# Cross attention in a decoder layer: transposing each head's probabilities as two row tiles, and a new order inside a slot

## What is computed

```python
q = _split_heads(query @ Wq.T + bq)          # 8 x 16 heads x 112 x 16
k = _split_heads(key @ Wk.T + bk)            # 8 x 16 heads x 375 x 16
v = _split_heads(value @ Wv.T + bv)
scores = jnp.einsum('bhqd,bhkd->bhqk', q, k) * scale
scores = jnp.where(mask == 0, NEG_INF, scores)
probs = jax.nn.softmax(scores, axis=-1)
out = jnp.einsum('bhqk,bhkd->bhqd', probs, v)
return out.transpose(0, 2, 1, 3).reshape(query.shape[0], -1, D_MODEL) @ Wo.T + bo
x = _layernorm(x + that)
```

## Time and profile before

| | |
|---|---|
| median of three runs | 433.10 us |
| profiled execution | 433.16 us |
| its span from first to last instruction | 431.4 us |
| TensorE busy with matmuls | 410.7 us, 95% |
| VectorE busy | 243.3 us, 56% |
| ScalarE busy | 193.9 us, 45% |
| cross attention, from 161.7 us on, to the last values at 328.4 us | about 167 us |

### The profile page before, as it was taken

How to read it: one execution, slowest core, us unless ns; L and a number is a source line. 1 busy time by engine, 2 the same in 40 slices (tenths; PEclk the granted TensorE clock), 3 DMA queues, 4 the chain that set the end, 5 groups by cost and what they waited for, 6 DMA issues and landing times.

```text
span 431.4 us, 8964 instructions
## 1 busy us (share of the span) xinstructions
PE 410.7 (95%) x3128; PEld 296.3 (69%) x3129; DVE 243.3 (56%) x724; ACT 193.9 (45%) x580; POOL 51.0 (12%) x77
## 2 busy tenths in 40 slices
PE   8999999999999979999999999999989999999992
PEld 7767879778796856776776676676665475666661
DVE  1275765747466566666675667666764642244443
ACT  1164362443526446677566666666683101111220
POOL 4010010100101001000010101010100054212222
PEclk9999999999999999999999999999999999999998
DMA  8999000000000013040404040920000013112210
GB/s 246 374 388 260 6 2 2 0 2 2 1 2 0 2 37 147 2 183 2 184 2 183 11 175 7 364 107 2 2 2 2 1 62 98 57 59 65 70 41 27
DMA packets 15242, 34.25 MB, mean 79 GB/s; under 512 B 2382, under 2 KB 9151, under 8 KB 13921
## 3 DMA queue, kind: packets, MB, share of 16 engines
q1 hardware_dynamic: 13952, 30.72, 20.4%
q0 software_dynamic: 1104, 2.76, 1.8%
q10 hardware_dynamic: 144, 0.23, 0.2%
HBM read 27.27 MB, written 6.70 MB: 79 GB/s over the span
## 4 chain that ended last, share of the span: by engine, by line
PE 88%; DVE 5%; ACT 4%; issue 2%; POOL 0%; POOLq 0%; DVEq 0%; ACTq 0%
PE bank L434 11%; PE bank L633 11%; PE bank L448 7%; PE bank L615 6%; PE bank L504 6%; PE bank L809 6%; PE bank L532 5%; PE bank L649 4%; PE bank L899 4%; PE bank L875 4%; PE bank L881 4%; PE bank L526 4%; PE bank L465 3%; PE bank L491 3%; PE bank L821 3%; PE bank L477 3%
## 5 line engine op out<-in xcount | busy, mean ns | idle before, releaser
L1255 DVE CUSTOM_DVE_ANT_0 p<-bank,mask 112x375 f32<-112x375 f32 x128 | 62.6, 544 | 36.5 <-PE bank L615 36.5
L1015 ACT ACTIVATE p<-p,nm 112x375 f32<-112x375 f32 x128 | 74.8, 609 | 2.0 <-DVE nm L1255 2.0
L633 PEld LDWEIGHTS bank<-ident,p 112*125 112x125 f32 x384 | 48.9, 187 | 22.9 <-issue 14.5
L1022 ACT ACTIVATE pT<-bank 125x336 f32<-125x336 f32 x96 | 42.9, 448 | 46.0 <-PE bank L633 46.0
L633 PE MATMUL bank<-ident,p 112*125 112x112 f32 x384 | 58.8, 286 | 1.0
L434 PE MATMUL bank<-x2T,arena 128*128 128x224 f32 x256 | 53.6, 357 | 0.0
L958 ACT ACTIVATE p<-bank,nm 112x112 f32<-112x112 f32 x128 | 43.7, 366 | 18.3 <-DVE nm L1126 18.2
L434 PEld LDWEIGHTS bank<-x2T,arena 128*128 128x128 f32 x256 | 47.0, 192 | 0.6 <-DMA x2T<-in_xT 0.5
L349 POOL TENSOR_TENSOR rstd<-veps,minus_half 128x1 f32<-128x1 f32 x14 | 7.7, 551 | 290.4 <-DVE veps L1152 290.4
L1126 DVE TENSOR_REDUCE nm<-bank 112x4 f32<-112x448 f32 x32 | 19.1, 619 | 24.1 <-PE bank L465 24.1
L615 PE MATMUL bank<-kT,qz 32*112 32x375 f32 x256 | 28.8, 517 | 3.6 <-ACT x2T L984 2.1
(11 more groups left out here) (143 smaller groups left out, 593.0 us busy)
## 6 DMA issues: line engine op xcount, KB each, us to landing
arena<-in_ug SPq DMA_DIRECT2D x8, 1024.0 KB, 5.6
arena<-in_dn SPq DMA_DIRECT2D x8, 512.0 KB, 6.8
mid<-in_ctxT SPq DMA_DIRECT2D x8, 375.0 KB, 3.1
slots_s<-blank SPq DMA_DIRECT2D x14, 128.5 KB, 3.9
arena<-in_wqk SPq DMA_DIRECT2D x7, 256.0 KB, 6.1
slots_x<-blank SPq DMA_DIRECT2D x14, 128.0 KB, 7.2
p<-slots_s SPq DMA_DIRECT2D x9, 128.5 KB, 2.0
kT<-slots_x SPq DMA_DIRECT2D x9, 128.0 KB, 2.1
```

Of the source, the lines that this page charges most:

```text
L633: mm = pe.transpose(PE_T2[r][0:SK, t * S:(t + 1) * S], p2[i % RING][:, t * SK:(t + 1) * SK], ident[0:S, 0:S])
L1015: act.activation(p2[i % RING], p2[i % RING], ACT.Exp, bias=nm2[:, i % H:i % H + 1], scale=-1.0).then_inc(exp2, 1)
L1022: act.activation(pT2[0:SK, i % RING], PE_T2[r][0:SK, 0:KT * S].rearrange("p (k n) -> p k n", k=KT), ACT.Copy).then_inc(pt2_act, 1)
L1255: v.tensor_tensor_reduce(p2[i % RING], PE_S2[r][0:S, 0:S2], bias[:], 1.0, 3e38, ALU.add, ALU.min, accum_out=nm2[:, i % H:i % H + 1]).then_ ...
```

## The change

Four things are changed, all in the cross attention and the few microseconds behind it.

1. Each transpose becomes two: queries 0 to 63 in the upper half of the array's rows (row tile at 0), queries 64 to 111 in the lower half (row tile at 64). The two write to different banks. A slot has 24 transposes in place of 12. Heads are taken in pairs `p`: pair 0 uses banks 4 and 7, pair 1 banks 0 and 1, and a bank holds one half of two heads: 2 x 3 x 64 = 384 columns or 2 x 3 x 48 = 288.
2. ScalarE evacuates both 64-query halves and one 48-query half, VectorE the other 48-query half.
3. The order in a slot is now scores, values, all transposes, all fills. ScalarE's order is: exponentials 0 and 1, two evacuations, exponential 2, an evacuation, exponential 3, and then evacuations of fills.
4. Two fills of the first sequence and the query projections use a second lent score bank, bank 3 (`PE_R2`), and the scores wait for these too. The first part of the second layer norm on VectorE is split: the addition stays at the start of a sequence's first slot, the moments go to the end of that slot. Behind the last slot, parts of the shared expert's first matmuls stand between the remaining steps, and the router's first logits come later.

```diff
-        PE_T2 = (bank[4], bank[7], PE_S2[0], PE_S2[1])
-        PE_L2 = PE_S2[2]
+        PE_T2 = ((bank[4], bank[7]), (PE_S2[0], PE_S2[1]))
+        PE_L2, PE_R2 = PE_S2[2], PE_S2[3]
+        HALVES = ((0, 64), (64, S))
...
-            def turn2_(n, r):
-                pe.wait_ge(exp2, n * STRIPS + r + 1)
+            def turn2_(n, p):
+                pe.wait_ge(exp2, n * STRIPS + 2 * p + 2)
...
+                elif p == 0:
+                    pe.wait_ge(pt2_act, 3 * n)
                 elif n + 1 < SLOTS:
-                    pe.wait_ge(max2, (n + 1) * STRIPS + r - 1)
-                i = n * STRIPS + r
-                for t in range(KT):
-                    mm = pe.transpose(PE_T2[r][0:SK, t * S:(t + 1) * S], p2[i % RING][:, t * SK:(t + 1) * SK], ident[0:S, 0:S])
+                    pe.wait_ge(max2, (n + 1) * STRIPS + 2)
+                for j in range(2):
+                    i = n * STRIPS + 2 * p + j
+                    for t in range(KT):
+                        for half, (q0, q1) in enumerate(HALVES):
+                            at = (j * KT + t) * (q1 - q0)
+                            mm = pe.transpose(PE_T2[p][half][0:SK, at:at + q1 - q0],
+                                              p2_all[q0:q1, (i % RING) * S2 + t * SK:(i % RING) * S2 + (t + 1) * SK],
+                                              ident[q0:q1, q0:q1])
                 mm.then_inc(turn2, 1)
...
+                if g == 1:
+                    pe.wait_ge(x1t_sb, 3)
+                    turn_x1(3)
+                    pe.wait_ge(max2, 4 * STRIPS // 2)
+                    turn_x1(4, PE_R2)
...
                 if n >= 2:
-                    pe.wait_ge(pt2_act, (n - 1) * 3)
+                    pe.wait_ge(pt2_act, 3 * (n - 2) + 2)
                     pe.wait_ge(pt2_dve, n - 1)
...
+                if g == 2 and b in (2, 4):
+                    pe.wait_ge(q_sb, b // 2 + 2)
+                if g in (2, 3) and b == 0:
+                    pe.wait_ge(x1t_sb, g + 3)
...
             for n in range(SLOTS):
                 score2(n)
+                if n >= 2:
+                    value2(n - 2)
                 if n >= 1:
                     turn2_(n - 1, 0)
                     turn2_(n - 1, 1)
-                between(n, 0)
-                if n >= 1:
-                    turn2_(n - 1, 2)
-                    turn2_(n - 1, 3)
-                between(n, 1)
-                between(n, 2)
-                if n >= 2:
-                    value2(n - 2)
+                fills(n)
...
+            shared(0, 0, range(0, 1))
             value2(SLOTS - 1)
-            logits_first()
+            shared(0, 0, range(1, 2))
+            turn_x2(NT - 2, bank[1])
             pe.wait_ge(y2, NT - 1)
             turn_o(B - 1)
-            shared(0, 0, range(0, 1))
+            shared(0, 1, range(0, 1))
             turn_on(B - 1)
-            shared(0, 0, range(1, 2))
+            shared(0, 1, range(1, 2))
+            logits_first()
             out2(NT - 1)
-            shared(0, 1)
             shared(1, 0)
...
             for n in range(SLOTS):
-                before_exps(n)
+                exps2(n, 0)
+                exps2(n, 1)
                 if n >= 1:
                     evac_pt(n - 1, 0)
-                exps2(n, 0)
+                    evac_pt(n - 1, 1)
+                amid(n)
+                exps2(n, 2)
                 if n >= 1:
-                    evac_pt(n - 1, 1)
-                exps2(n, 1)
-                between(n, 0)
-                if n >= 1:
-                    evac_pt(n - 1, 2)
-                exps2(n, 2)
-                between(n, 1)
+                    evac_pt(n - 1, 0, 1)
                 exps2(n, 3)
+                after(n)
...
                 if (g, place) == (0, 0) and b >= 3:
-                    ln2_a(b - 3)
+                    ln2_add(b - 3)
                 if (g, place) == (0, 3) and b >= 1:
                     evac_v(2, b, PE_L2)
+                if (g, place) == (0, 4) and b >= 3:
+                    ln2_a(b - 3)
```

More of the change, by code:

```diff
@@ L690, in between_first, with fills @@
                     project_q(1)
-                if (g, place) == (2, 2):
+                    pe.wait_ge(max2, 3 * STRIPS)
+                    turn_x1(5, PE_R2)
+                if g == 3:
                     pe.wait_ge(q_sb, 2)
-                    turn_x1(5)
-                if (g, place) == (3, 0):
-                    pe.wait_ge(x1t_sb, 6)
                     turn_x1(6)
-            def between(n, place):
+            def fills(n):
                 b, g = n // GROUPS, n % GROUPS
-                if place == 1:
+                if (g == 0 and b >= 1) or (g >= 2 and b + 1 < B) or (g == 1 and b >= 3):
@@ L731, in between @@
-                if (g, place) == (2, 1) and b + 1 < B:
-                    project_v(0, b + 1, PE_L2)
-                if (g, place) == (3, 0) and b >= 1:
-                    turn_on(b - 1)
-                if (g, place) == (3, 1) and b + 1 < B:
-                    project_v(1, b + 1, PE_L2)
-                if (g, place) == (3, 2) and b >= 2:
-                    out2(b - 2)
+                if g == 0 and b >= 1:
+                    project_v(2, b, PE_L2)
+                    if b + 1 < B:
+                        if b == 1:
+                            pe.wait_ge(x1t_sb, NT)
+                        elif b == 2:
+                            pe.wait_ge(ont_sb, 1)
+                        else:
+                            pe.wait_ge(y2, b - 2)
+                        project_k(0, b + 1)
@@ new lines, in fills @@
+                if g == 1 and b >= 1:
+                    if b >= 3:
+                        turn_x2(b - 3)
+                    if b in (2, 4):
+                        pe.wait_ge(max2, n * STRIPS + 4)
+                        project_q(b // 2 + 1, PE_R2)
+                    if b + 1 < B:
+                        pe.wait_ge(k_sb, (b + 1) * KC + 1)
+                        project_k(1, b + 1)
+                if g == 2:
+                    if b + 1 < B:
+                        project_v(0, b + 1, PE_L2)
+                    if b >= 1:
+                        if b + 1 < B:
+                            pe.wait_ge(k_sb, (b + 2) * KC)
+                        else:
+                            pe.wait_ge(y2, B - 3)
+                        turn_o(b - 1)
@@ L740, in lent_banks_back @@
+                if g == 3:
+                    if b >= 1:
+                        turn_on(b - 1)
+                    if b + 1 < B:
+                        project_v(1, b + 1, PE_L2)
+                    if b >= 2:
+                        out2(b - 2)
+                if b == 0:
+                    first_fills(g)
             def lent_banks_back(n):
@@ L1023, in evac_pt, with amid @@
                                ACT.Copy).then_inc(pt2_act, 1)
[L1025 removed]
+            def amid(n):
                 b, g = n // GROUPS, n % GROUPS
[L1028 to L1047 removed]
+                if g == 1 and b >= 3:
+                    evac_x2(b - 3)
+                if g == 3 and b >= 1:
+                    evac_on(b - 1)
@@ L1049, in _, with after @@
+            def after(n):
+                b, g = n // GROUPS, n % GROUPS
+                if n < GROUPS:
+                    for t in ((2,), (3, 4), (5,), (6,))[n]:
+                        evac_x1(t, PE_R2 if t in (4, 5) else PE_M2)
+                if g < 2 and 1 <= b < B - 1:
+                    evac_k(g, b + 1)
             for n in range(SLOTS):
-                before_exps(n)
+                exps2(n, 0)
+                exps2(n, 1)
                 if n >= 1:
                     evac_pt(n - 1, 0)
-                exps2(n, 0)
+                    evac_pt(n - 1, 1)
+                amid(n)
+                exps2(n, 2)
@@ L1068, in evac_logits @@
+            evac_x2(NT - 2, bank[1])
             def evac_logits():
@@ L1145, in layernorm_a, with moments @@
                 v.tensor_tensor(ybuf[:, p], src, xb[:, p], ALU.add).then_inc(sy, 1)
+            def moments(b, p, sy, ss, sa, sv):
                 v.wait_ge(sy, b + 1)
@@ L1154, in ln1_a @@
             def ln1_a(t):
-                layernorm_a(PE_W1[:, 0:C], wout1, xb1, t, t % 2, y1, st1, ag1, ve1)
+                add_rest(PE_W1[:, 0:C], wout1, xb1, t, t % 2, y1)
+                moments(t, t % 2, y1, st1, ag1, ve1)
             def ln1_b(t):
@@ L1252, in mask_and_max @@
                 if i >= RING:
-                    v.wait_ge(turn2, i - RING + 1)
+                    v.wait_ge(turn2, 2 * (n - 2) + r // 2 + 1)
                 v.sem_inc(pause, 1)
```

114 lines of the change are left out of this document (31 added, 83 removed).

## The result

The changed kernel takes 447.42 us (median of 4 runs, 446.83 to 448.02) against 433.37 us before: ratio 1.032, interval 1.031 to 1.034. The forecast was 434.3 us with a range up to 437.4, so the sign of the likeliest case was right and its size, and the range, were wrong. The profiled execution took 448.02 us with a span of 446.3, which is 14.9 us more than before.

What follows compares the result with a forecast made beforehand. TensorE's instruction list plus its short waits was taken as the bound. Sequences 1 to 6 -1.88, sequence 0 +2.08, sequence 7 and the end +0.92: +1.1 on 433.16, so 434.3 us, 8-in-10 range 430.6 to 437.4.

Steps and rivals of the forecast that it cites:

- The transposes: Twelve tiled pairs replace twelve single transposes in a slot; a pair was taken at 0.109 us, no gain.
- The change of shape: Between transposes and fills, a slot's fourth change of array shape was to cost 0.15 us.
- The way from a release to TensorE's load: Waits after a release: 0.03 us before the second pair of heads, 0.04 for a passage from evacuation to scores.
- the first slots' -0.38: First slot of a sequence: 5.36 us instead of 5.74, waits of 0.56 gone and 0.2 paid for shape.
- The late layer norm: Moments moved to the first slot's end delay the next slot's strips: +0.15 us in second slots, +0.26 in slot 29.
- The query evacuations of sequences 2 and 4: Second slots wait for lent bank 3, evacuated 6.37 and 6.55 us after slot start: +0.18 and +0.38.
- Slot 1: Slot 2's scores wait until ScalarE has evacuated transposed x1 block 4 from bank 3: +1.63 us.
- The end: From slot 31's start to the last x2 transpose: 18.1 us instead of 17.7, +0.44.
- Gates that don't bind: Rival: block 4, query and value evacuations and late moments come in time; 3.5 us less, 430.8 us; chance 0.25.
- ScalarE as the slower chain: Rival: an exponential costs 0.60 us, not 0.50; fourth slots, slot 1 and end move, about +3, 437.3 us; chance 0.15.
- The other three: Rivals: halves gain from streaming less, 420 us, 0.05; halves' loads take turns, 475, 0.03; free change of shape, 428.4, 0.04.
- the rival of a free change of shape: Rival: changing shape between transposes and fills costs nothing, 5.9 us less, 428.4 us; chance 0.04.

Runs made afterwards that it cites:

- the two mended kernels: Changed order with whole-array transposes, x1 blocks 4 and 5, late wait and layer norm step moved later: 430.73 us; same with tiles: 433.4 to 434.2 or 438.0 to 438.9.
- the twins: The 430.73 us kernel with whole-array transposes, and the same with row tiles put back, 433.4 to 434.2 us in seven runs, 438.0 to 438.9 in three.
- the three pairs of twins: Tiles against whole array: on the 430.73 us kernel; 438.37 (block 4 late, idle work) against 434.74 us; changed kernel 447.42 against 436.84 us.
- 434.74, 433.47 and at last 430.73 us: Changed kernel with whole-array transposes and x1 block 4 in slot 2; then late wait last; then layer norm 2's last step and x1 block 5 later.

## Why the prediction was wrong

The forecast came out at +1.1 us where +14 were measured. Point by point, in its own steps:

**The clock (8.1 us, in no term and no rival).** The prediction counted every slot at the granted clock of 1.00 that the trace of before has, and it forecast a wait of 1.6 us in slot 1 without asking what TensorE's clock does after it. This is the step that failed, and the largest part of the miss. Idle work in the pauses gives 8.1 us back and changes next to nothing else, so the price of the clock is shown. Its cause is shown in part: the forecast wait of slot 1 lies behind the start of the first fall, pauses of 0.3 to 1.1 us stand ahead of both, and filling the three at slots 28 and 29 removes the second. Why tiled transposes make the clock fall where whole-array ones don't is not shown, only that they do: 10.24 and 10.24 us at half against 3.4 us, at the same pauses.

**The transposes: right.** The pair's distance is 0.108 to 0.109, as taken from the self attention's pairs; neither the half stream nor loads in turns. The Trainium skill, "TensorEngine Tiling (Array Packing)", section Theoretical Speedup, gives up to 2x for a small dimension of at most 64; the comparison of the two mended kernels shows 3.4 us lost instead.

**The change of shape: right.** 0.15 was taken for transposes to fills, 0.18 was measured between the twins.

**The way from a release to TensorE's load: the term that was mis-sized.** I took 0.03 for the wait before the second pair of heads and 0.04 from evacuation to scores. They are 0.11 and 0.24. A load came 0.12 after what released it where the late wait stood last, and 0.22 to 0.24 where one more stood behind it; putting the late one last took 0.11 off. That is 0.08 in nearly every slot, which turned the first slots' -0.38 into -0.30, and 0.2 more in each slot that the value projection gates. The terms named for the evacuation in the third slot also add up to 4.58, where the sum goes on with 4.66. Over sequences 1 to 6 the sum was to be -1.88 and is +2.3.

**The late layer norm: right gate, half its size.** It was put at +0.15 for the second slots and +0.26 for slot 29. In the second slot of sequence 5 the strips begin 280.86 - 279.32 = 1.54 us after the scores' load, not 1.30:

```profile
280.86 0.54 DVE L1252 CUSTOM_DVE_ANT_0 p<-bank,mask 112x375 f32<-112x375 f32 x1
```

Moving it gave 0.32 back in the second slots and 0.94 in slot 29. The query evacuations of sequences 2 and 4 ended at 6.27 and 6.75 against 6.37 and 6.55 forecast, and the scores followed 0.22 later: slots of 6.49 and 6.97.

**Slot 1: right.** +1.63 forecast, +1.72 measured, with the x1 evacuation as releaser (the row of slot 2's first matmul ends in `[1.73 <-ACT x1T L975]`). The sum of the earlier trace rows held.

**The end.** +0.44 was forecast for slot 31 to the last x2 transpose. Measured +1.42, but in the kernel with idle work it is 17.75 us against 17.66 before, and the way from slot 31 to the end of the span is 112.9 us, as before (112.85): all but 0.1 of it was the clock, and the +0.44 isn't there.

**The rivals.** Gates that don't bind: false for block 4, the query evacuations, the value projection and the late layer norm. ScalarE as the slower chain: false, fourth slots are 5.21 against the 5.16 forecast. The other three are excluded by the pair distance and the change of shape. With the clock held up, the changed kernel is at 439.3, also above the range: without the fall the mis-sized waits and gates alone would have left the forecast short by 5 us. Two slips in the working change nothing of this: the rival of a free change of shape takes off 0.19 a slot where the sum holds 0.15, so 4.7 us and not 5.9, and the shares named for the chances give 0.54 for slower and 0.18 for the same, where 0.51 and 0.21 stand.

The 14 us in all: 8.1 clock; 3.4 to 3.9 tiles (the three pairs of twins: 157.5 against 154.1, 161.4 against 157.6, and 0.10 to 0.16 a slot in the third); the remaining 2 to 2.5 us are gates of the new order, which can be mended: 434.74, 433.47 and at last 430.73 us with the same order.

## What to carry to other kernels

When a change adds waits to TensorE or makes its instructions smaller, look at the granted clock behind them: here each of two falls cost about 4 us, among pauses of about 1 us, and that price doesn't stand in any duration of the kernel before. Look also at when the clock falls: the longest pause here came after the fall had begun. Splitting a transpose into row tiles saved nothing here: each tile still loads its full width of weight columns, a pair's distance stayed that of one whole load (0.108 to 0.109), and a change of shape came on top; compare load distances, not stream lengths. Where an engine waits for several things, put the one that comes last at the end of the list.

## What the runs showed of the hardware that I had not expected

- In the changed kernel the pauses ahead of both falls of the clock were only 0.3 to 1.1 us. Each fall lasted 10.24 us and cost about 4 us: 3.8 in slot 2, 2.8 + 1.4 around slot 30.
- At the half clock, pairs of tiled transposes and the values take 1.7 to 1.8 times as long (24 loads 2.60 instead of 1.52, values 0.95 instead of 0.54 us).
- With tiles, the same program can hold the clock in one execution and lose it in the next (ten runs: 433.4 to 434.2 and 438.0 to 438.9). The median hides that.
- TensorE's load followed what released it by 0.12 us, and by 0.22 to 0.24 where one more wait stood behind the late one. The difference is about a whole transpose's distance.
